# A W4 macaron block on one core: gate and up scale and zero tables loaded in TensorE's row layout, the first layer norm in halves

## The chip, the cores and the metric

One core of a Trainium2 chip runs the whole program. The metric is the device time of one execution in microseconds (us), as the median of several runs. TensorE (PE in the rows, PEld for its weight loads), VectorE (DVE), ScalarE (ACT), GpSimd (POOL) and the queue of SyncE (SP) each work through their own instructions in order and wait for each other on semaphores. A trailing q, as in SPq or ACTq, marks what a sequencer does itself, above all issuing a DMA.

## What is computed

The input x is 2048 tokens of 512 numbers. It passes a feed-forward block, an attention layer and the same feed-forward block again, each behind a layer norm and each added back:

```python
x = x + 0.5 * ffn(layernorm(x))
x = x + attn(layernorm(x))
x = x + 0.5 * ffn(layernorm(x))
```

The feed-forward weights are 4-bit numbers, eight in one int32, with one scale and one zero for each group of 128 input rows and each output column:

```python
w = (qw[:, None, :] >> shifts[None, :, None] & 15).reshape(-1, n)        # HID 512, INTER 1376
z = ((qz[:, :, None] >> shifts[None, None, :] & 15) + 1).reshape(groups, -1)
W = (w - z[g_idx]) * scales[g_idx]
h = silu(xf @ Wg) * (xf @ Wu)
out = h @ Wd
```

Gate and up have 4 groups (GK), down has 10 (GD). The index g_idx may name any group for any input row, so a row's scale has to be looked up.

## The kernel before

**Where the work is.** The 2048 rows are four blocks of 512 for the two feed-forward passes. Block 0 and block 1 of the first pass ("pair 0") go through plain_top and plain_bottom. While plain_top runs, the weights are unpacked too. All matrix products are made of three passes over a high and a low part of each number, so a 128x512 product over 512 input rows is 12 matmuls.

**Units.** The weights are unpacked in 33 units, a unit being one 128-column tile of gate (m = 0) or up (m = 1), or one 128-row tile of down (m = 2). Their order is gate 0, up 0, then for every i from 1 gate i, up i, down i-1. Gate and up have 11 tiles (NT). For unit u:

- the queue brings the packed words into the tile qs (load_units, L490), VectorE shifts and masks them in place (unpack, L1703)
- TensorE makes the zeros and scales of the unit with scales_zeros(u) (L816 for gate and up, L814 for down): a one-hot matrix oh_gu or oh_d times a table tab_gu or tab_d. This waits until VectorE is done with unit u-1 (s_wf)
- dequantise(u) on VectorE subtracts the zeros (wi, L1619) and multiplies by the scales (wf, L1720)
- ScalarE copies wf to the high part (w_hi, L1245) and GpSimd makes the low part (w_lo, L2109). TensorE may then multiply with it (s_wlo)

**The tables.** A table has for each matrix 3 rows per group with the three bf16 parts of the scale, and from row 32 on one row per group with the zeros. Up's rows start at 64 (FOLD). Before, scales and zeros are loaded spread over many partitions (sc_gu, zq_gu), GpSimd cuts the scales in three parts (cut_scales, 5 instructions), VectorE unpacks the zeros (unpack_zeros, 8 shifts and one sum), and 8 DMAs of the SP queue (table, L418 and L421) carry the pieces across partitions into tab_gu. Down's tables take the same way, with the zeros unpacked by VectorE as its first work.

**The start.** In program order TensorE does keep_warm(4), that is 4 products of the identity that nobody reads, scales_zeros(0), the turning of x's first two 128-row tiles (L1030), scales_zeros(1), the other two, scales_zeros(2) and keep_warm(4), and then plain_top. keep_warm is at L743 and waits at the start for the identity and the column shift (d_small). VectorE makes the layer norm's statistics (ln_stats, ln_var), GpSimd the power -1/2 (deviation), ScalarE applies it (ln_apply, L1250).

**plain_top on TensorE.** For every tile i: 12 matmuls of gate, scales_zeros(3i+2), 12 of up, scales_zeros(3i+3), 12 of down for tile i-1, scales_zeros(3i+4). VectorE does dequantise(3i+2), the product with silu (hs, L1745), dequantise(3i+3), the low part of hT, dequantise(3i+4). For i = 0 VectorE has units 2 to 5 in it, and the one-hot of down's first tile; for i = 1 the one-hot of the other tiles (128x640). GpSimd prepares these one-hots between its w_lo of units 2 and 4 (L452, L455).

## Time and profile before

| | us |
|---|---|
| median of 3 runs | 856.06 |
| lowest and highest | 855.16, 857.8 |
| the profiled execution | 854.81 |
| its span, as in the page | 853.0 |
| TensorE busy in that span | 829.8 |

The profiled execution has 1.81 us outside its span. A row of the timeline is: start, duration, engine, line, operation, output<-inputs, shapes, count, and in brackets how long the engine had been idle and what ended that. Rows of the same kind are merged, and a merged duration runs from the first start to the last end.

### The profile page before, as it was taken

The numbers are of one execution on the slowest core, as the hardware profiler recorded it, in microseconds if no ns is written. First come the engines' busy times: TensorE is split into PE (matmuls) and PEld (weight loads), VectorE is DVE, ScalarE is ACT, GpSimd is POOL, SyncE is SP. The second block draws the span as 40 slices with busy tenths as digits, with TensorE's granted clock in tenths as the row PEclk, the third lists the DMA queues.
The fourth block names the chain that finished last, engine by engine and source line by source line (L and its number), as shares of the span: only waits on it lengthen the run. The fifth ranks groups of instructions, "written<-read, shape, count | busy, mean of one in ns | idle before, by whom it ended". The sixth has DMA issues, their size and how long they took to land.

```text
span 853.0 us, 10668 instructions
## 1 busy us (share of the span) xinstructions
PE 829.8 (97%) x4004; PEld 674.2 (79%) x4004; DVE 481.9 (56%) x798; ACT 272.3 (32%) x469; POOL 243.8 (29%) x198
## 2 busy tenths in 40 slices
PE   2999999999999999999999999999999999999998
PEld 2777768887888888788888888888888888888786
DVE  4877655564845444464967786545445744434452
ACT  2323332354421121241574783111212512111221
POOL 4544431563210533030235362150510201101100
PEclk9999999999999999999999999999999999999999
DMA  6767556995484534152115156845345063544121
GB/s 153 215 231 245 185 178 229 337 325 209 171 313 136 173 127 147 50 161 88 61 68 179 50 172 247 309 136 173 125 149 165 22 226 132 163 146 153 35 100 50
DMA packets 72290, 139.37 MB, mean 163 GB/s; under 512 B 25566, under 2 KB 36494, under 8 KB 67246
## 3 DMA queue, kind: packets, MB, share of 16 engines
q1 hardware_dynamic: 66236, 130.79, 45.6%
q10 hardware_dynamic: 5874, 7.48, 2.8%
q8 instruction: 32, 0.52, 0.3%
q0 software_dynamic: 128, 0.41, 0.3%
q14 instruction: 20, 0.16, 0.1%
HBM read 100.54 MB, written 37.95 MB: 162 GB/s over the span
## 4 chain that ended last, share of the span: by engine, by line
PE 73%; DVE 2%; ACT 1%; issue 0%; POOL 0%; DVEq 0%; ACTq 0%; POOLq 0%
PE ps L729 37%; PE ps L736 33%; PE ps L747 2%; PE ps L1130 1%; DVE xn L1651 1%; DVE pT L1619 0%; ACT pr L1479 0%; POOL t L2109 0%; ACT oT L1245 0%; DVE oT L1619 0%; DVE t L1619 0%; DVE hT L1619 0%; PE ps L1056 0%; DVE mx L1946 0%; ACT xn L1250 0%
## 5 line engine op out<-in xcount | busy, mean ns | idle before, releaser
L729 PE MATMUL ps<-blk,ring 128*128 128x512 f32 (+1 forms) x1386 | 320.9, 389 | 0.1
L729 PEld LDWEIGHTS ps<-blk,ring 128*128 128x128 f32 (+1 forms) x1386 | 256.7, 185 | 58.1 <-DVE blk L1619 0.5
L736 PE MATMUL ps<-wd,hT 128*128 128x512 f32 (+1 forms) x1056 | 251.1, 392 | 0.9 <-DVE hT L1619 0.8
L736 PEld LDWEIGHTS ps<-wd,hT 128*128 128x128 f32 (+1 forms) x1056 | 196.8, 188 | 43.8 <-DVE hT L1619 1.2
L2151 POOL TENSOR_TENSOR h<-h,u 128x512 f32<-128x512 f32 (+1 forms) x33 | 42.7, 1293 | 326.0 <-ACT h L1372 326.0
L736 PE MATMUL ps<-xT,wp 128*128 128x512 f32 x480 | 115.8, 396 | 0.0
L736 PEld LDWEIGHTS ps<-xT,wp 128*128 128x128 f32 x480 | 88.5, 188 | 21.2 <-issue 2.0
L1622 DVE TENSOR_TENSOR u<-ps,p1s 128x512 f32<-128x512 f32 (+1 forms) x66 | 45.4, 687 | 97.3 <-PE ps L729 97.3
L1372 ACT ACTIVATE h<-h 128x512 f32<-128x512 f32 (+1 forms) x33 | 20.9, 632 | 176.8 <-DVE h L1622 176.8
L1622 DVE TENSOR_TENSOR u<-ps,u 128x512 f32<-128x512 f32 (+1 forms) x66 | 45.6, 691 | 25.7 <-PE ps L729 24.6
L1622 DVE TENSOR_TENSOR h<-ps,p1s 128x512 f32<-128x512 f32 (+1 forms) x33 | 22.8, 691 | 64.1 <-PE ps L729 64.1
L1619 DVE TENSOR_TENSOR hT<-h,hT 128x512 fp32r<-128x512 f32 (+1 forms) x44 | 30.7, 712 | 24.8 <-ACT hT L1245 24.8
L1367 ACT ACTIVATE g<-ps 128x512 f32<-128x512 f32 (+1 forms) x33 | 19.7, 598 | 76.1 <-PE ps L729 76.1
L1245 ACT ACTIVATE hT<-u 128x512 fp32r<-128x512 f32 (+1 forms) x33 | 20.9, 632 | 64.4 <-DVE u L1835 64.4
L1835 DVE TENSOR_TENSOR u<-u,g 128x512 f32<-128x512 f32 (+1 forms) x33 | 38.8, 1174 | 1.1
L2119 POOL TENSOR_SCALAR xn<-xn,mv,rstd 128x512 f32<-128x512 f32 x18 | 38.3, 2136 | 0.5
L1245 ACT ACTIVATE hT<-h 128x512 fp32r<-128x512 f32 (+1 forms) x44 | 27.0, 629 | 35.5 <-PE ps L736 35.5
L2109 POOL TENSOR_TENSOR wp<-wf,wp 128x512 fp32r<-128x512 f32 x20 | 26.9, 1344 | 40.1 <-ACT wp L1245 40.0
L1619 DVE TENSOR_TENSOR hT<-u,hT 128x512 fp32r<-128x512 f32 (+1 forms) x33 | 22.8, 692 | 23.0 <-ACT hT L1245 23.0
L2114 POOL TENSOR_TENSOR rstd<-rstd,mhalf 128x4 f32<-128x4 f32 x12 | 15.2, 1267 | 66.9 <-DVE rstd L1640 66.9
L1619 DVE TENSOR_TENSOR wi<-qs,ps 128x512 bf16<-128x512 int32 (+2 forms) x33 | 22.3, 676 | 19.1 <-PE ps L816 13.8
L1860 DVE SCALAR_TENSOR_TENSOR xres<-ps,xres 128x512 f32<-128x512 f32 x32 | 21.6, 689 | 18.6 <-PE ps L736 18.5
(123 smaller groups left out, 876.7 us busy)
## 6 DMA issues: line engine op xcount, KB each, us to landing
ring<-wsaved SPq DMA_DIRECT2D x29, 1024.0 KB, 5.1
ring<-wsaved SPq DMA_DIRECT2D x33, 768.0 KB, 4.4
wsaved<-wp SPq DMA_DIRECT2D x10, 1024.0 KB, 4.7
stream<-xres SPq DMA_DIRECT2D x32, 256.0 KB, 2.2
xn<-stream SPq DMA_DIRECT2D x8, 1024.0 KB, 7.8
xres<-stream SPq DMA_DIRECT2D x32, 256.0 KB, 4.0
wfull<-wf ACTq DMA_DIRECT2D x20, 256.0 KB, 3.3
wsaved<-wp SPq DMA_DIRECT2D x10, 512.0 KB, 3.0
```

Source lines behind the costliest of these rows:

```text
L729: mm = pe.matmul(ps[0:w, bank, :], ring[:, slot, which, a, kt, 0:w], blk[:, which, b, kt, :], start=not onto and kt == 0 and n == 0, stop= ...
L736: mm = pe.matmul(bank_ap, lhs(a), rhs(b), start=first and n == 0, stop=last and n == 2)
L1245: return act.activation(dst, src, ACT.Copy)
L1367: act.activation(g1[0:w, n % 2, :], ps[0:w, product_bank(n // NT + 1, 0), :], ACT.Silu).then_inc(s_g1, 1)
L1372: act.activation(hidden(i)[0:width(i), :], hidden(i)[0:width(i), :], ACT.Silu).then_inc(s_g2, 1)
L1619: return dve.tensor_tensor(out=dst, in0=a, in1=b, op=ALU.subtract)
L1622: return dve.tensor_tensor(out=dst, in0=a, in1=b, op=ALU.add)
L1835: dve.tensor_tensor(out=u2[0:w, n % 2, :], in0=u2[0:w, n % 2, :], in1=g1[0:w, n % 2, :], op=ALU.mult)\
L1860: dve.scalar_tensor_tensor(out=xres[:, r, :], in0=ps[:, down_bank(q, half, r), :], scalar=0.5, in1=xres[:, r, :], op0=ALU.mult, op1=ALU.ad ...
L2109: return pool.tensor_tensor(out=dst, in0=a, in1=b, op=ALU.subtract)
L2119: pool.tensor_scalar(x_rows(t)[:, r, :], x_rows(t)[:, r, :], mv[:, t % 2, r, 0:1], rstd[:, t % 2, r:r + 1], ALU.subtract, ALU.mult).then_i ...
L2151: pool.tensor_tensor(out=hidden(i)[0:w, :], in0=hidden(i)[0:w, :], in1=u3[0:w, n % 2, :], op=ALU.mult).then_inc(s_h2, 1)
```

## The change

**Loads.** The SP queue now loads the indices first, then zq_gu as 4 rows for each matrix straight into the rows of the table, and sc_gu three times over as 12 rows for each matrix. GpSimd clears both tiles first, and SP waits for that. The rows between are thus zero.

**Tables made in place.** VectorE makes the tables in three pieces of columns: tiles 0 and 1 (256 columns) at the start, tiles 2 to 4 (384) in plain_top with i = 0, tiles 5 to 10 (736) with i = 2. For a piece, zeros_gu is 8 shifts and one sum on 100 partitions, and scales_gu two scalar_tensor_tensor on 76 partitions. They subtract the upper half of the float, or not, by a constant keep for each row, and TensorE reads the upper 16 bits of what is left (upper, a step of two bf16). The 8 table DMAs for gate and up are gone, and GpSimd's 5 cuts for them too. TensorE waits for a piece (s_tab) ahead of the first unit of its tiles.

**Down.** Unpacking down's zeros moves from VectorE's first work to plain_top, i = 0, behind the first one-hot. Its DMA into tab_d follows that. GpSimd's clamp and compare for down move from the start to just ahead of w_lo(2).

**The start.** Normalising x's first block goes in halves on VectorE, GpSimd and ScalarE. TensorE makes 12 warm-up products at the start instead of 4, turns all four tiles of x in one go, makes scales_zeros(1) and scales_zeros(2) behind them, and the 4 warm-up products ahead of plain_top are gone. ScalarE's queue brings unit 0 right behind x, and SP's brings unit 1.

```diff
-        def unpack_zeros(eng, step, sc, rest, rest2, parts, zq, zi, zb):
+        def unpack_zeros(eng, step, zq, zi, zb):
...
+        def scales_gu(eng, step, piece):
...
+            first, end = TAB_TILES[piece][0] * P, min(TAB_TILES[piece][1] * P, INTER)
+            s, left, dst = sc_gu[S_ROWS, first:end], left_gu[S_ROWS, 0:end - first], tab_gu[S_ROWS, first:end]
+            step(lambda: eng.scalar_tensor_tensor(out=left, in0=upper(s), scalar=keep[S_ROWS, 0:1], in1=s,
+                                                  op0=ALU.mult, op1=ALU.subtract))
+            step(lambda: eng.scalar_tensor_tensor(out=dst, in0=upper(left), scalar=keep[S_ROWS, 1:2], in1=left,
+                                                  op0=ALU.mult, op1=ALU.subtract))
...
             sp.dma_start(idt[:, :], ident).then_inc(d_small, 16)
             sp.dma_start(shift[:, :], shifts).then_inc(d_small, 16)
-
-
-            for j in range(3):
-                sp.wait_ge(s_cut, 2 * j + 1)
-                for m in range(2):
-                    table(sp, m, pieces=(j,))
-            sp.wait_ge(s_tab, 2 * ZERO_STEPS)
-            for m in range(2):
-                table(sp, m, pieces=(3,))
+            load_units(sp, [1])
+            sp.dma_start(zq_d, flat(zeros[2], ZC_D)).then_inc(d_zq_d, 16)
             load_units(sp, [2, 3])
-            sp.wait_ge(s_cut, 2 * CUT_STEPS)
-            table(sp, 2)
+            sp.wait_ge(s_cut, CUT_STEPS)
+            table_d(sp, 0, range(3))
             load_units(sp, [4, 5])
+            sp.wait_ge(s_tab, ZEROS_D_DONE)
+            table_d(sp, 0, (3,))
...
+                if m == 0:
+                    for piece, (first, _) in enumerate(TAB_TILES):
+                        if i == first:
+                            pe.wait_ge(s_tab, TAB_DONE[piece])
...
             pe.wait_ge(d_small, 32)
-            keep_warm(4)
-
-            pe.wait_ge(d_tab[0], 64)
-            pe.wait_ge(s_oh, 3)
+            keep_warm(12)
+
+            pe.wait_ge(s_oh, 2)
             scales_zeros(0)
             for r in range(RT):
-                if r == 2:
-                    pe.wait_ge(d_tab[1], 64)
-                    scales_zeros(1)
                 pe.wait_ge(s_ln[0], r + 1)
...
+            scales_zeros(1)
             scales_zeros(2)
-            keep_warm(4)
...
                     if i == 0:
-                        dve.wait_ge(s_ohd, 2)
+                        dve.wait_ge(s_ohd, 3)
                         one_hot(dve, hots, DOWN_FIRST, 1, oh_d[:, 0:P])
+                        unpack_zeros(dve, tables, zq_d, zi_d, zb_d.rearrange("p c j -> p (c j)"))
                         dequantise(3)
...
+                    if i == 2:
+                        zeros_gu(dve, tables, 2)
+                        scales_gu(dve, tables, 2)
...
                     if i == 0:
                         dequantise(4)
+                        zeros_gu(dve, tables, 1)
+                        scales_gu(dve, tables, 1)
                         dequantise(5)
```

VectorE in plain_top, i = 0, from unit 4 on, before (wi and wf belong to dequantise, qs to unpack, hs and hT to the hidden tile):

```order
L1619 TENSOR_TENSOR hT<-hs,hT 128x512
L1619 TENSOR_TENSOR wi<-qs,ps 128x512
L1720 TENSOR_TENSOR wf<-wi,ps 128x512
L1703 TENSOR_SCALAR qs<-qs,shift 128x512
L1619 TENSOR_TENSOR wi<-qs,ps 128x512
```

The same stretch now:

```order
L1653 TENSOR_TENSOR hT<-hs,hT 128x512
L1653 TENSOR_TENSOR wi<-qs,ps 128x512
L1756 TENSOR_TENSOR wf<-wi,ps 128x512
L1739 TENSOR_SCALAR qs<-qs,shift 128x512
L460 TENSOR_SCALAR zi_gu<-zq_gu 100x48 x8
L462 TENSOR_SCALAR zb_gu<-zi_gu 100x384
L474 SCALAR_TENSOR_TENSOR left_gu<-sc_gu,keep 76x384
L476 SCALAR_TENSOR_TENSOR tab_gu<-left_gu,keep 76x384
L1653 TENSOR_TENSOR wi<-qs,ps 128x512
```

Eleven instructions stand between dequantise(4) and dequantise(5). The same eleven, with 92 and 736 columns, stand ahead of the hs of i = 2.

The SP queue from the constants on, before:

```order
L574 DMA idt<-in_ident 128x128
L575 DMA shift<-in_shifts 128x1
L418 DMA tab_gu<-parts_gu 4x32x43 x6
L421 DMA tab_gu<-zb_gu 4x4x344 x2
L490 DMA qs<-in_L_ffn_gate_qweight 128x1x128 x4
L490 DMA qs<-in_L_ffn_up_qweight 128x1x128 x4
L418 DMA tab_d<-parts_d 10x8x64 x3
L421 DMA tab_d<-zb_d 10x4x128
L490 DMA qs<-in_L_ffn_down_qweight 128x1x512
```

The same stretch now, behind the loads of idx, grp, zq_gu and sc_gu:

```order
L612 DMA idt<-in_ident 128x128
L613 DMA shift<-in_shifts 128x1
L522 DMA qs<-in_L_ffn_up_qweight 128x1x128 x4
L615 DMA zq_d<-in_L_ffn_down_qzeros 40x16
L522 DMA qs<-in_L_ffn_gate_qweight 128x1x128 x4
L522 DMA qs<-in_L_ffn_up_qweight 128x1x128 x4
L423 DMA tab_d<-parts_d 10x8x64 x3
L522 DMA qs<-in_L_ffn_down_qweight 128x1x512
L522 DMA qs<-in_L_ffn_gate_qweight 128x1x128 x4
L426 DMA tab_d<-zb_d 10x4x128
```

The transfers that VectorE's and GpSimd's cuts fed are gone from the front, and the one with down's zeros stands behind two more units.

## Rows read from the trace of the kernel before

**Rows 1.** The page: busy time by engine, share of the span and count.
```profile
PE 829.8 (97%) x4004; PEld 674.2 (79%) x4004; DVE 481.9 (56%) x798; ACT 272.3 (32%) x469; POOL 243.8 (29%) x198
```
**Rows 2.** Stretches: start:end, length, busy us by engine, granted clock, DMA share, GB/s.
```profile
35.00:45.00 10.00, 9.33 (x53) 6.87 (x46) 9.48 (x13) 3.40 (x6) 5.54 (x5) 1.00 0.97 309
45.00:115.00 70.00, 70.00 (x388) 49.63 (x386) 50.03 (x88) 24.09 (x39) 29.69 (x23) 1.00 0.69 228
```
**Rows 3.** The only wait of TensorE in 24.7 to 125 us: total, times, longest.
```profile
PE ps L814 <- DVE wf L1720: 0.7, 1, 0.7
```
**Rows 4.** Timeline of the start: tables and layer norm.
```profile
6.21 0.88 DVE L446 TENSOR_SCALAR zi_gu<-zq_gu 32x43 int32<-32x43 int32 x8 [0.41 <-DMA zq_gu<-in_L_ffn_up_qzeros]
7.12 0.33 DVE L448 TENSOR_SCALAR zb_gu<-zi_gu 32x344 bf16<-32x344 int32 x1
...
10.06 1.29 POOL L2114 TENSOR_TENSOR rstd<-rstd,mhalf 128x4 f32<-128x4 f32 x1 [1.16 <-DVE rstd L1640]
10.22 3.25 SPq L421 DMA_DIRECT2D tab_gu<-zb_gu  x2
...
11.53 0.74 DVE L458 SCALAR_TENSOR_TENSOR oh_gu<-idf,grp,oh_gu 128x512 bf16<-128x512 f32 x1
11.65 2.92 ACT L1250 ACTIVATE xn<-xn,nmr,rstd 128x512 f32<-128x512 f32 x4 [5.67 <-DVE nmr L1644]
```
**Rows 5.** Timeline of TensorE up to plain_top.
```profile
9.33 2.08 PE L743 MATMUL ps<-idt 128*128 128x128 f32 x8 [9.33 <-DMA shift<-in_shifts]
17.56 0.61 PE L816 MATMUL ps<-tab_gu,oh_gu 4*128 4x128 bf16 x8 [6.16 <-DMA tab_gu<-zb_gu]
20.54 1.97 PE L1030 MATMUL ps<-idt,xn 128*128 128x128 f32 x8
22.98 2.01 PE L743 MATMUL ps<-idt 128*128 128x128 f32 x8
24.71 4.41 PE L736 MATMUL ps<-xT,wp 128*128 128x512 f32 x18
```
**Rows 6.** Timeline: warm-ups and turning at another pace, later.
```profile
30.89 0.60 PE L743 MATMUL ps<-idt 128*128 128x128 f32 x4
127.82 1.04 PE L747 MATMUL ps<-idt,xn 128*128 128x128 f32 x8
```
**Rows 7.** Timeline of plain_top, i = 0 and 1: VectorE, GpSimd, TensorE.
```profile
20.72 0.69 DVE L1619 TENSOR_TENSOR wi<-qs,ps 128x512 bf16<-128x512 int32 x1 [0.64 <-PE ps L816]
24.56 1.28 POOL L2109 TENSOR_TENSOR wp<-wf,wp 128x512 fp32r<-128x512 f32 x1 [2.79 <-ACT wp L1245]
24.93 1.19 DVE L1703 TENSOR_SCALAR qs<-qs,shift 128x512 int32<-128x512 int32 x1
27.88 0.35 DVE L458 SCALAR_TENSOR_TENSOR oh_d<-idf,grp,oh_d 128x128 bf16<-128x128 f32 x1
34.03 0.69 DVE L1720 TENSOR_TENSOR wf<-wi,ps 128x512 f32<-128x512 bf16 x1
34.78 0.40 PE L816 MATMUL ps<-tab_gu,oh_gu 4*128 4x128 bf16 x8
38.00 1.90 DVE L458 SCALAR_TENSOR_TENSOR oh_d<-idf,grp,oh_d 128x640 bf16<-128x640 f32 x1
42.40 3.02 PE L736 MATMUL ps<-xT,wp 128*128 128x512 f32 x12
```
**Rows 8.** Timeline of i = 2.
```profile
47.19 0.48 DVE L1703 TENSOR_SCALAR qs<-qs,shift 128x512 int32<-128x512 int32 x1
48.02 1.28 POOL L2109 TENSOR_TENSOR wp<-wf,wp 128x512 fp32r<-128x512 f32 x1 [1.74 <-ACT wp L1245]
48.77 0.69 DVE L1745 TENSOR_TENSOR hs<-hs,ps 128x512 f32<-128x512 f32 x1 [1.10 <-PE ps L736]
50.09 0.69 DVE L1720 TENSOR_TENSOR wf<-wi,ps 128x512 f32<-128x512 bf16 x1
51.98 0.39 PE L814 MATMUL ps<-tab_d,oh_d 10*128 10x512 bf16 x2
```

More of the change, by code:

```diff
@@ L252, in macaron @@
         d_q = [sem(f"d_q{n}") for n in range(QSLOTS)]
-        d_tab = [sem(f"d_tab{n}") for n in range(4)]
+        d_tab = [sem(f"d_tab{n}") for n in range(2)]
         d_full = [sem(f"d_full{n}") for n in range(2)]
@@ L407, in spread, with table_d, upper @@
             return indices.rearrange("(o n) -> o n", o=1).to_broadcast([FOLD, indices.shape[0]])
-        def table(eng, m, at_row=0, pieces=range(4)):
-            if m == 2:
-                (_, _, _, parts, _, _, zb), dst, g, done = cuts[1], tab_d, GD, d_tab[3 if at_row else 2]
-            else:
-                (_, _, _, parts, _, _, zb), dst, g, done, at_row = cuts[0], tab_gu, GK, d_tab[m], FOLD * m
-                parts, zb = parts[:, :, m * SC:(m + 1) * SC], zb[m * ZP:(m + 1) * ZP, :, :]
+        def table_d(eng, at_row, pieces=range(4)):
+            done = d_tab[1 if at_row else 0]
             for j in [j for j in pieces if j < 3]:
-                eng.dma_start(dst[at_row + j * g:at_row + (j + 1) * g, :], parts[:, j, :]).then_inc(done, 16)
+                eng.dma_start(tab_d[at_row + j * GD:at_row + (j + 1) * GD, :], parts_d[:, j, :]).then_inc(done, 16)
             row = at_row + Z_ROW
             if 3 in pieces:
-                eng.dma_start(dst[row:row + g, :], zb.rearrange("p c j -> p (c j)")).then_inc(done, 16)
+                eng.dma_start(tab_d[row:row + GD, :], zb_d.rearrange("p c j -> p (c j)")).then_inc(done, 16)
+        def upper(ap):
+            return ap.bitcast(BF16)[:, 1::2]
         def maker(eng, semaphore):
@@ L595, in _ @@
                 if u == 9:
[L596 removed]
+                    table_d(sp, FOLD)
                 if u == 12:
@@ L815, in scales_zeros @@
                         else:
+                            cols = slice(i * P, i * P + w)
                             mm = pe.matmul(ps[:, bank, k * P:k * P + w], oh_gu[rows, k * P:(k + 1) * P],
-                                           tab_gu[rows, i * P:i * P + w], start=True, stop=True)
+                                           zb_gu[rows, cols] if bank == Z_BANK else upper(tab_gu[rows, cols]),
+                                           start=True, stop=True)
                 mm.then_inc(s_sz, 1)
@@ L1251, in ln_apply, with rows_hi @@
                                    scale=rstd[:, t % 2, r:r + 1]).then_inc(s_ln[t], 1)
-            def rows_hi(t):
-                for k in range(KT):
+            def rows_hi(t, kts=range(KT)):
+                for k in kts:
                     act.wait_ge(s_turn, KT * t + k + 1)
```

172 lines of the change are left out of this document (101 added, 71 removed).

## The prediction

> **What bounds the kernel now.** I read the page's busy times first: TensorE is busy for 829.8 of the 853.0 us of the span [rows 1], so the time is TensorE's, and what can be won is where it stands still, 23 us in all. Its timeline and the list of its waits say where: 9.33 us ahead of its first instruction, 6.16 us for the last piece of gate's table [rows 5], and 0.7 us for VectorE in plain_top [rows 3]. The table by stretches then tells who is near the limit behind the start. From 45 to 115 us TensorE is busy for 70.00 of 70.00 us and VectorE for 50.03; from 35 to 45 us it is the other way about, with VectorE at 9.48 of 10 us and TensorE at 9.33 [rows 2]. So there are two questions. When does the first product of plain_top start (24.71 us now [rows 5]), and does VectorE keep up behind it, now that it is to make the tables there?
>
> **The start.** Now TensorE does its warm-ups at 9.33 us and then waits for a table until 17.56 us [rows 5]. The table is late since SP issues its last two transfers from 10.22 us on for 3.25 us [rows 4], and they have to land. These go away. What is late next is, in turn:
>
> The constants. The first warm-up waits for the shift, which is there at 9.33 us [rows 5]. In the new order SP has 256 KB of indices and the scales, three times over, in front of it and waits for two memsets of GpSimd, which no row shows; on the other hand 6 of the 8 table transfers no longer crowd in behind it. I take 9.3 us again, from 8.5 to 10.5.
>
> The warm-ups. Four take 2.08 us at the start (8 records [rows 5]) and two take 0.60 us later (4 records [rows 6]), so 12 take 6.2 us at the slow pace and 3.6 at the fast one. The eight records ahead of plain_top still take 2.01 us at 22.98 us [rows 5]: the clock is at the lower of its two levels (1.2 GHz) until plain_top, although the granted clock reads 1.00 in all rows. I take 5.7 us, most of them slow, and so 15.0 us for the end of the warm-ups.
>
> VectorE and ScalarE are ready by then. For piece 0 VectorE has 8 shifts (0.88 us for 43 columns, so no more for 32) and a sum (0.33 us for 344 columns, 0.29 for 256 [rows 4]), and two scalar_tensor_tensor. Their price is that of the one-hot: 0.74 us for 512 columns [rows 4], which with VectorE's other one (0.35 us for 128 columns [rows 7]) makes 0.21 us and 1.04 ns for each column, so 0.48 us for 256. With statistics, one-hot and waits this ends near 12.5 us. The second power of GpSimd (1.29 us [rows 4]) ends near 12, and ScalarE's four tiles (2.92 us [rows 4]) near 14.2 us.
>
> Then scales_zeros(0), 0.5 us, and 16 turnings. They take 1.97 us for 8 at the slow pace [rows 5] and 1.04 at the fast one [rows 6]: I take the fast one, 2.1 us, since TensorE has been busy for 6 us without a gap, and keep the slow one (1.9 us more) for the range. With scales_zeros(1) VectorE's dequantise(1) starts at about 18.1 us. Before, it started at 20.72 us [rows 7]. The first product came 3.99 us after that, held back by the four warm-ups in front of it. Now it only waits for the first row tile's low part: 0.72 + 0.61 + 0.69 + 0.1 = 2.1 us, so 20.2 us. **The start gives 4.5 us.**
>
> **The tables in plain_top, i = 0.** Now dequantise(4) ends at 34.03 + 0.69 = 34.72 us, and scales_zeros(5) starts at 34.78 us [rows 7]: already here TensorE follows VectorE. In the new program scales_zeros(5) is the first that reads piece 1, so it waits for eleven more instructions, and what is queued behind it are gate's, up's and down's products. VectorE's chain from the start of dequantise(1), from start to start in the rows' durations: wi and wf 1.33, four low parts of x 2.48, unpack(2) 0.48, dequantise(2) with unpack(3) 1.81, one-hot 0.35, down's zeros 0.97 (8 shifts and a sum, as they take now at the start), dequantise(3) 1.81, hs and hT with ScalarE's copy between them 2.07, dequantise(4) 1.81, zeros of piece 1 1.2 (8 times 0.1, and 0.36 for 384 columns), its scales 1.25 (2 times 0.61). The sum is 15.6 us.
>
> This chain has no slack that takes waits for GpSimd in. A row shows what such a wait is: the unpack at 24.93 us takes 1.19 us instead of 0.48, and it ends at 26.12, that is 0.28 us after GpSimd's w_lo of 24.56 to 25.84 us; the one-hot at 38.00 us takes 1.90 us [rows 7] instead of 0.88. So such an instruction of VectorE waits for the w_lo that is under way. A w_lo starts some 0.8 us after its wf ends (48.02 us, behind an unpack that started at 47.19 us as wf ended [rows 8]), and for units 2 and 4 that is now in the midst of the new instructions. The bounds are 0 (they just miss) and 3.3 us (three w_lo of 1.28 us, less 0.5 us that they overlap anyhow). I take 1.9 us, nearer to the upper end, since with units 2 and 4 the times fall together by the sum. **Piece 1 is ready 17.5 us after dequantise(1), at 35.6 us, and scales_zeros(5) starts at 35.7 us, 0.9 us later than now.** The 4.5 us are gone: TensorE has done what it can 10.1 us after its first product (34.78 - 24.71 [rows 5, 7]), at 30.3 us, and stands still for some 5.3 us.
>
> Down's table is not what is late. Its zeros are ready at about 26.5 us, the transfer takes some 2.1 us to land (bounds 2 and 4.5 us, the table transfers of the start), and scales_zeros(4) is due at 28.3 us. Up to 2 us of wait there would only shorten the wait behind it.
>
> Behind it, before, TensorE needs 42.40 - 34.78 = 7.62 us to gate's product of i = 2, of which 0.7 us is a wait for VectorE [rows 3, 7], whose long one-hot came ahead of hs. Now VectorE has that one-hot done while TensorE is still in up's products, and I take 0.2 us for the rest of the wait: 35.7 + 7.15 = 42.85 us. **At i = 2 the kernel stands 0.45 us later than before.**
>
> **The tables at i = 2.** The third piece is 8 shifts of 92 words (0.11 us each), a sum (0.53 for 736 columns) and two scalar_tensor_tensor (0.98 each): 3.5 us with their gaps. They stand between the unpack at 47.19 us and hs at 48.77 us, where VectorE is idle for 1.10 us. Behind hs, dequantise(9) ends at 50.78 us, 1.20 us ahead of scales_zeros(10) at 51.98 us [rows 8]. So 2.3 us are covered and 1.2 us are not. With GpSimd's w_lo of unit 8 in it, at about 48 us, it is 2.2 us. I take 1.6 us. All later pieces of work have their cover: VectorE has 50.03 us of work in 70 us [rows 2]. **Here 1.6 us are lost.**
>
> **Sum.** +0.45 + 1.6 = +2.0 us against the profiled execution of 854.81 us. That execution lies 1.25 us below the median of 856.06 us, and I put the difference on the median: 858.1 us, 0.2% more. Differences within 0.3% (2.6 us) are about what a measurement of this kernel can't tell from no change.
>
> **Rivals.**
>
> *The clock falls in the new wait (slower).* Up to 24.7 us rows show TensorE at its lower level, after it stood still from 11.41 to 17.56 us [rows 5]; no row has it stand still for more than 0.7 us once it is at 2.4 GHz [rows 3]. The new wait for piece 1 is about 5.3 us, in the midst of plain_top. If the clock falls there, the same work takes twice as long until it rises again. TensorE worked at the slow pace from 17.56 to 24.7 us [rows 5] before it ran fast, so I price it with 2 to 7 us of slow work, of which half is lost, 1.0 to 3.5 us, and take 2.5: 860.6 us. It decides by the wait at scales_zeros(5): one of 0.7 us leaves the clock up, one of 5.3 us may not. The Trainium skill says on the page TensorE: Matmul & The Clock Gate, in the section "Why this matters for your kernels", that gaps in TensorE's work between bursts of matmuls bring it back to the lower clock; by that page the forecast would be this rival and not the even case, while no run here shows it yet.
>
> *VectorE is through earlier (faster).* If the new instructions miss GpSimd's w_lo and the constants land at 8.5 us, the table is ready at 32.9 us instead of 35.6 us, and at i = 2 1.2 us are lost instead of 1.6. That would be -3 us; with one of the two, -1. I take 854.6 us, from 851.5 to 856.3. For it speaks that the rows have only one such wait for certain between 24 and 30 us [rows 7].
>
> *The start stays slow.* The turning of x at the slow pace makes all of it 1.9 us later, or the constants land after 10.5 us: 860 us. A table read in steps of two bf16 that slowed its 4 products in each unit would also give this: one product is 0.40 / 8 = 0.05 us [rows 7], so 0.2 us in each of some 17 units, 3.4 us.
>
> **How the numbers follow.** Even case with its 2.0 us: 40%, of which 27% end within 2.6 us. The clock falls: 20%, nearly all of it slower. VectorE through earlier: 30%, 17% below -2.6 us and 13% within. Slow start or slow table: 10%, 8% slower. Together faster 17%, the same 43%, slower 40%. The range leaves out about a tenth at each end: 853.0 to 862.0 us.
>
> **What the changed profile would show.** First product of plain_top at about 20 us. TensorE waits for VectorE at scales_zeros(5) for 4 to 6 us, with the eleven instructions at 30 to 36 us. The warm-ups of the start change their pace within the twelve. gate's product of i = 2 at about 43 us, and ahead of scales_zeros(10) a wait of 1 to 2 us. The busy time of TensorE behind 55 us is as before. The prediction is wrong if the wait at scales_zeros(5) is under 2 us, if the first product starts after 22 us, or if products behind that wait run at half their pace.

## The result: 0.6% slower, and the profile after

The changed kernel takes 862.09 us in the median of 4 runs (862.04 to 862.29), the kernel before 856.81 us beside it (4 runs, 855.16 to 857.8): a ratio of 1.0064 with a 95% interval of 1.0046 to 1.0082. It is slower by 5.3 us. The forecast was 858.1 us, and the time lies just outside its range, whose upper end was 862.0 us. Nothing in the forecast's likeliest case had the size of this; the nearest case was the first rival, the falling clock, at 860.6 us.

The profiled execution after is one of 862.04 us, 7.2 us above the one of before (854.81 us); the working below is against that one. First its page's busy times, and all waits of TensorE in the first 130 us (total, times, longest):

```profile
PE 833.5 (97%) x4012; PEld 677.5 (79%) x4012; DVE 486.7 (57%) x824; ACT 272.4 (32%) x469; POOL 248.7 (29%) x202
```

```profile
PE ps L776 <- DMA shift<-in_shifts: 11.0, 1, 11.0
PE ps L854 <- DVE tab_gu L476: 4.6, 1, 4.6
PE ps L851 <- DVE wf L1756: 2.3, 1, 2.3
PE ps L854 <- DVE wf L1756: 1.6, 1, 1.6
PE ps L769 <- DVE xT L1653: 0.3, 1, 0.3
```

The 6.16 us of wait for a table at the start [rows 5] are gone. In their place there are 4.6 us for VectorE's table work at scales_zeros(5), 2.3 us at scales_zeros(10), and 1.6 us at scales_zeros(2), where before the only wait in plain_top was one of 0.7 us [rows 3]. TensorE is also busy for 3.7 us more than before [rows 1], of which the 4 more products of the identity explain 0.6 us (12 in 4.71 us, 8 in 2.08 + 2.01 us before [rows 5]). The timeline of TensorE tells why (warm-ups L776, turnings L1065, products L769, scales_zeros L854 and L851):

```profile
11.04 4.71 PE L776 MATMUL ps<-idt 128*128 128x128 f32 x24 [11.04 <-DMA shift<-in_shifts]
16.01 1.97 PE L1065 MATMUL ps<-idt,xn 128*128 128x128 f32 x16
20.57 5.97 PE L769 MATMUL ps<-xT,wp 128*128 128x512 f32 x18 [0.29 <-DVE xT L1653]
...
36.82 0.28 PE L854 MATMUL ps<-zb_gu,oh_gu 4*128 4x128 bf16 x1 [4.62 <-DVE tab_gu L476]
37.35 5.19 PE L769 MATMUL ps<-xT,wp 128*128 128x512 f32 x12
42.81 3.02 PE L769 MATMUL ps<-wd,hT 128*128 128x512 f32 x12
46.08 3.06 PE L769 MATMUL ps<-xT,wp 128*128 128x512 f32 x12
57.99 0.39 PE L851 MATMUL ps<-tab_d,oh_d 10*128 10x512 bf16 x2 [2.30 <-DVE wf L1756]
```

The first product starts at 20.57 us instead of 24.71 us [rows 5], so the new start is worth 4.1 us. But its first 18 matmuls take 5.97 us, where they took 4.41 us [rows 5], and the 12 of up's product at 37.35 us take 5.19 us, where such a product takes 3.02 us elsewhere. The table by stretches has the reason in its column for the granted clock (the last but two):

```profile
21.60:25.00 3.40, 3.40 (x10) 2.63 (x9) 3.30 (x11) 0.00 (x0) 1.68 (x3) 0.50 0.49 139
25.00:35.20 10.20, 7.19 (x39) 4.92 (x37) 8.05 (x26) 3.49 (x6) 8.49 (x5) 1.00 0.49 146
35.30:42.00 6.70, 5.18 (x19) 4.04 (x20) 4.00 (x6) 0.63 (x1) 1.99 (x2) 0.50 0.76 249
42.10:59.10 17.00, 14.70 (x81) 10.26 (x81) 14.06 (x28) 4.39 (x7) 4.82 (x4) 1.00 0.60 193
59.20:62.50 3.30, 3.30 (x10) 2.52 (x8) 1.41 (x3) 0.63 (x1) 2.15 (x2) 0.50 0.45 118
```

TensorE works at 1.2 GHz (0.50) in three stretches: from 21.6 us, shortly after the wait of 1.6 us; from 35.3 us, in the wait of 4.6 us; and from 59.2 us, shortly after the wait of 2.3 us. Before, the clock reads 1.00 from the first product to 35 us, and behind that too [rows 2]:

```profile
24.70:35.00 10.30, 10.30 (x60) 7.53 (x59) 8.10 (x14) 2.63 (x5) 6.97 (x5) 1.00 0.68 200
```

VectorE's eleven instructions for piece 1, and GpSimd beside them:

```profile
32.05 0.96 DVE L1739 TENSOR_SCALAR qs<-qs,shift 128x512 int32<-128x512 int32 x1
32.93 0.85 DVE L460 TENSOR_SCALAR zi_gu<-zq_gu 100x48 int32<-100x48 int32 x8
33.82 0.75 DVE L462 TENSOR_SCALAR zb_gu<-zi_gu 100x384 bf16<-100x384 int32 x1
34.60 1.51 DVE L474 SCALAR_TENSOR_TENSOR left_gu<-sc_gu,keep 76x384 f32<-76x384 bf16 x1
36.15 0.61 DVE L476 SCALAR_TENSOR_TENSOR tab_gu<-left_gu,keep 76x384 f32<-76x384 bf16 x1
...
31.94 2.41 POOL L483 TENSOR_SCALAR oh_d<-idf,grp 128x640 bf16<-128x640 f32 x1
34.44 1.26 POOL L2156 TENSOR_TENSOR wd<-wf,wd 128x512 fp32r<-128x512 f32 x1
```

left_gu takes 1.51 us and tab_gu 0.61 us for the same 384 columns. The first of them ran beside GpSimd's w_lo of 34.44 to 35.70 us.

**Where 7.2 us come from.** Step by step along TensorE's path, in us, profiled executions:

| | before | after | grows by |
|---|---|---|---|
| scales_zeros(5) starts | 34.78 | 36.82 | 2.0 |
| from there to gate's product of i = 2 | 7.62 | 9.26 | 1.6 |
| wait at scales_zeros(10) | none | 2.30 | 2.3 |
| gate's product of i = 3 | 3.06 | 4.61 | 1.6 |

That is 7.5 us, against 7.2 us at the end. The second row hides a part of the clock's price: the 7.62 us before hold the wait of 0.7 us [rows 3], and the 9.26 us after hold none. So TensorE's own work on that way grew by 2.3 us, 2.2 us of it in up's product (5.19 against 3.02 us). With the 1.6 us of the last row the lower clock costs 3.9 us in this execution. Behind it nothing changes: from 125 us to 850 us TensorE is busy for 721.39 us of 725 after and for 720.97 us before.

### The profile page after: what moved, and what is told of

It reads as the page before. It is cut to its first block, busy times and chain, and to the rows that moved or that the text cites. A ratio compares the mean times of both kernels' runs of the same rounds, so it can differ in the third digit from the quotient of the medians.

```text
span 860.2 us, 10709 instructions
## 1 busy us (share of the span) xinstructions
PE 833.5 (97%) x4012; PEld 677.5 (79%) x4012; DVE 486.7 (57%) x824; ACT 272.4 (32%) x469; POOL 248.7 (29%) x202
## 4 chain that ended last, share of the span: by engine, by line
PE 72%; DVE 2%; ACT 1%; issue 0%; POOL 0%; DVEq 0%; ACTq 0%; POOLq 0%
PE ps L762 36%; PE ps L769 33%; PE ps L780 2%; PE ps L1165 1%; DVE xn L1687 1%; DVE pT L1653 0%; ACT pr L1513 0%; POOL t L2156 0%; ACT oT L1280 0%; DVE oT L1653 0%; DVE t L1653 0%; DVE hT L1653 0%; PE ps L1091 0%; DVE mx L1993 0%; ACT xn L1285 0%
## 5 line engine op out<-in xcount | busy, mean ns | idle before, releaser
L769 PE MATMUL ps<-wd,hT 128*128 128x512 f32 (+1 forms) x1056 | 250.8, 392 | 0.8 <-DVE hT L1653 0.7
L769 PEld LDWEIGHTS ps<-wd,hT 128*128 128x128 f32 (+1 forms) x1056 | 196.8, 188 | 43.5 <-DVE hT L1653 1.1
L769 PE MATMUL ps<-xT,wp 128*128 128x512 f32 x480 | 120.8, 409 | 0.3 <-DVE xT L1653 0.3
L769 PEld LDWEIGHTS ps<-xT,wp 128*128 128x128 f32 x480 | 92.4, 196 | 22.9 <-issue 2.7
L2161 POOL TENSOR_TENSOR rstd<-rstd,mhalf 128x4 f32<-128x4 f32 (+1 forms) x13 | 15.5, 1196 | 67.5 <-DVE rstd L1675 67.5
L1902 DVE SCALAR_TENSOR_TENSOR xres<-ps,xres 128x512 f32<-128x512 f32 x32 | 21.6, 690 | 18.8 <-PE ps L769 18.5
```

The lines of the kernel that those rows point to most:

```text
L769: mm = pe.matmul(bank_ap, lhs(a), rhs(b), start=first and n == 0, stop=last and n == 2)
L1902: dve.scalar_tensor_tensor(out=xres[:, r, :], in0=ps[:, down_bank(q, half, r), :], scalar=0.5, in1=xres[:, r, :], op0=ALU.mult, op1=ALU.ad ...
```

## Experiments

Two theories are on trial. *A: the new waits for table work and the lower clock behind them are the whole loss.* *B: a part of it lies in something else: the new start, the table read in steps of two, or waits that turn up wherever the work is put.* The kernels before ran on the same chips: 855.11 us (7 runs) beside the first four, 855.34 us (29) beside the next four, 855.82 us (18) beside the last three. The intervals in the table are those of the ratios to these. The changed kernel wasn't run again beside them: its ratio is to the 856.81 us of its own 4 runs, and the later medians of the kernel before are 1.0 to 1.7 us lower. So a difference of two medians and a difference of two ratios don't say the same, and where it matters both are given. One of e10_fill's ten executions took 2816.43 us, for a reason that no run shows; the ratio leaves it out, and without it the median is 858.54 us.

| run | median us | ratio, 95% | first product | scales_zeros(5) | wait there | lower clock (us) |
|---|---|---|---|---|---|---|
| changed kernel | 862.09 | 1.0046 to 1.0082 | 20.57 | 36.82 | 4.62 | 3.4 + 6.8 + 3.4 |
| e1_warm_wait | 860.76 | 1.0049 to 1.0112 | 21.18 | 37.43 | 1.53 | 3.4 + 3.5 |
| e2_warm_start | 862.65 | 1.0074 to 1.0116 | 21.09 | 37.59 | 5.64 | 6.8 + 3.4 |
| e3_split_last | 861.29 | 1.0058 to 1.0098 | 21.33 | 37.84 | 5.65 | 6.9 |
| e4_zd_front | 861.87 | 1.0068 to 1.0107 | 21.05 | 37.31 | 4.63 | 3.4 + 6.9 + 3.5 |
| e5_spread | 856.43 | 1.0001 to 1.0025 | 20.94 | 32.54 | none | 3.4 + 3.4 |
| e6_warm_zd | 859.35 | 1.0032 to 1.0071 | 21.94 | 36.62 | 4.68 | 6.8 + 3.4 |
| e10_fill | 858.70 | 1.0024 to 1.0050 | 20.90 | 37.70 | 0.74 | 3.5 |
| e11_early_hot | 859.91 | 1.0028 to 1.0069 | 21.36 | 35.69 | 3.99 | 6.8 + 3.4 |
| e8_best | 852.65 | 0.9960 to 0.9985 | 18.94 | 28.98 | none | none |
| e9_slots | 849.77 | 0.9918 to 0.9951 | 20.75 | 30.80 | none | none |

Marks and stretches are from the one profiled execution of each run; "lower clock" lists how long each stretch at 1.2 GHz lasted. The shift lands between 9.4 and 11.8 us from run to run, so marks of two runs compare to some 0.5 us only.

### The clock alone: warm-up products in the waits

```diff
+                    if i == 1:
+                        warm(14, 7)
                     scales_zeros(3 * i + 2)
```

> The changed kernel with 14 more warm-up products (into a bank that is free then) ahead of scales_zeros(5), so that TensorE is busy while it waits for piece 1 of the tables; nothing else is changed. Theory A (the clock falls because TensorE stands still for 4.6 us there, and that costs time): the granted clock stays at 1.00 from 35 to 42 us, the way from scales_zeros(5) to gate's product of i = 2 shrinks from 9.26 us to 7.1 to 7.3 us, and the time falls by about 2 us, to 860.0 us. Theory B (only the wait itself costs; the slow work of TensorE lies beside VectorE's): the clock stays up, but gate's product of i = 2 starts at 46.0 us as before and the time stays at 862.1 us. In both, piece 1 is ready at 36.8 us.

Products of the identity fill two thirds of the wait. The clock falls later and for half as long, for 3.5 us; gate's product of i = 2 comes 8.43 us behind scales_zeros(5) instead of 9.26 us. In this execution the clock also stayed up behind the wait of 2.29 us at i = 2, which the edit doesn't touch: gate's product of i = 3 takes 3.06 us instead of 4.61 us.

```profile
58.09 3.06 PE L769 MATMUL ps<-xT,wp 128*128 128x512 f32 x12
```

The median of 860.76 us is 1.3 us below the changed kernel's, but the four executions reach from 859.4 to 863.73 us and the interval of the ratio overlaps that of the changed kernel, so this run alone shows no gain. A wait of 1.53 us was still left. So both waits were then filled nearly whole:

```diff
+                    if i == 1:
+                        warm(20, 7)
                     scales_zeros(3 * i + 2)
...
+                        if i == 2:
+                            pe.wait_ge(s_silu, 3)
+                            warm(10, 0)
                         scales_zeros(3 * i + 4)
```

> The changed kernel with 20 warm-up products ahead of scales_zeros(5) and 10 ahead of scales_zeros(10), so that both waits are filled nearly whole; the tables are where the change put them. This takes the lower clock away and leaves the waits. Theory A (behind the two waits the clock costs 1.6 us each): scales_zeros(5) and scales_zeros(10) start when VectorE is done, as in the changed kernel, granted clock 1.00 from 25 us on, gate's product of i = 2 7.0 to 7.6 us behind scales_zeros(5) instead of 9.3 us, and 3 us less in all, 859 us. Theory B (what follows the waits is slow for another reason, or warm-ups don't hold the clock): low clock in the same places and 862 us, or more, since the warm-ups overrun the waits.

```profile
26.00:60.00 34.00, 32.77 (x204) 25.52 (x202) 27.64 (x54) 8.33 (x14) 16.01 (x11) 1.00 0.62 201
```

The clock is 1.00 from 26 to 60 us, gate's product of i = 2 comes 6.89 us behind scales_zeros(5) (44.59 - 37.70), and that of i = 3 takes 3.04 us. Together that is 2.4 + 1.6 = 4.0 us less, about the 3.9 us worked out above. The median falls by 3.4 us to 858.7 us, with VectorE's work just where the change put it; by the ratios it is 2.3 us (1.0037 against 1.0064). So the clock behind the two waits costs 2.3 to 4 us, and theory A's 3 us lie within. The remaining 2.9 us above the kernel before (858.70 against 855.82 us) fit the waits themselves.

### VectorE's chain: what makes piece 1 late

```diff
             scales_zeros(1)
+            warm(5, 0)
             scales_zeros(2)
```

> The changed kernel with 5 more warm-up products between scales_zeros(1) and scales_zeros(2), where TensorE waits 1.6 us for VectorE. Theory A (the low clock of 21.6 to 25.0 us comes from the thin work of TensorE between the warm-ups and the first product, and it holds VectorE up by 1.3 us at dequantise(3)): the clock stays at 1.00 until the long wait, the first 18 matmuls take 4.5 us instead of 5.97, piece 1 is ready at 35.5 us instead of 36.8, and the time is 860.8 us. Theory B (the slow products lie in the shadow of VectorE, which is the bound): piece 1 is ready at 36.8 us again and the time stays at 862.1 us.

The lower clock behind the first product goes, and the first 18 matmuls take 4.36 us. It gains nothing at all: scales_zeros(5) starts no earlier and waits 1.0 us longer. The trace shows why. VectorE's wait of 1.28 us for TensorE ahead of dequantise(3) is gone, but the eight shifts of down's zeros take 2.36 us instead of 0.73 us. GpSimd's low part falls among them now, at 25.39 us; in the changed kernel it starts at 26.45 us, behind them:

```profile
25.26 2.36 DVE L460 TENSOR_SCALAR zi_d<-zq_d 40x16 int32<-40x16 int32 x8
...
25.39 1.28 POOL L2161 TENSOR_TENSOR wp<-wf,wp 128x512 fp32r<-128x512 f32 x1 [1.40 <-ACT wp L1285]
```

So 1.28 us are won and 1.6 us lost. Neither of the two theories of this run had that. Down's zeros alone, unpacked at the start again:

```diff
+            dve.wait_ge(d_zq_d, 16)
+            unpack_zeros(dve, tables, zq_d, zi_d, zb_d.rearrange("p c j -> p (c j)"))
             dve.wait_ge(d_zq_gu, 32)
             zeros_gu(dve, tables, 0)
```

> The changed kernel with down's zeros unpacked at the start again, while VectorE waits for gate's and up's zeros (their load goes ahead of theirs). Theory A (VectorE's chain from dequantise(1) to piece 1 is the bound, every instruction in it counts): piece 1 is ready 1.0 us earlier after dequantise(1), at 35.8 us, and the time falls by 1 us to 861.1 us, if the start isn't held up. Theory B (TensorE's slow products set the chain: VectorE waits 1.28 us for them at dequantise(3)): VectorE just waits 2.2 us there, piece 1 is ready at 36.8 us and the time stays at 862.1 us.

Nothing either: scales_zeros(5) starts at 37.31 us, since VectorE now waits 2.29 us instead of 1.28 us for scales_zeros(3), behind TensorE's slow first 18 matmuls. Each of the two edits hides the other's gain: without the warm-ups VectorE waits for TensorE, and with them down's zeros meet GpSimd. Together:

> The changed kernel with five warm-up products between scales_zeros(1) and scales_zeros(2) and with down's zeros unpacked in the start again; piece 1 stays where it is. Theory A (VectorE's own chain from dequantise(1) to piece 1 sets the end of the wait; its idle 1.3 us ahead of dequantise(3) came from TensorE at the lower clock, and down's zeros cost 1.0 us more): piece 1 is ready 16.0 to 16.5 us after the start of dequantise(1) instead of 18.3 us, scales_zeros(5) at 35 to 35.5 us with a wait of 4 to 5 us, and the lower clock behind it stays: about 860 us. Theory B (each relief is eaten by a wait for GpSimd's low parts, which the chain then meets elsewhere): still 18 us or more, and 862 us.

Piece 1 is ready 16.8 us after the start of dequantise(1) (19.79 to 36.56 us) instead of 18.3 us, and the median is 859.35 us. On the same chip that is 3.3 and 2.5 us less than with either edit alone. Against the changed kernel it is 2.7 us less by the medians and 1.1 us by the ratios (1.0051 and 1.0064). The expected 16.0 to 16.5 us was missed a little: VectorE still waits 0.66 us for TensorE. On top of this, GpSimd's 640 columns of one-hot were moved ahead of its low parts of units 2 and 3, away from piece 1:

```diff
                     compare_low(pool, hots, DOWN_FIRST, 1, oh_d[:, 0:P])
-                if u == 3:
                     clamp(pool, hots, DOWN_REST, GD)
-                if u == 4:
+                if u == 3:
```

> The changed kernel with five warm-up products between scales_zeros(1) and scales_zeros(2), down's zeros in the start, and one more move: GpSimd prepares the one-hot of 640 columns ahead of its low parts of units 2 and 3 instead of those of units 3 and 4, so that it doesn't work beside VectorE's unpacking for unit 5 and the eleven instructions of piece 1. Theory A (VectorE's instructions that take 0.97 instead of 0.48, 0.75 instead of 0.36 and 1.51 instead of 0.61 us wait for GpSimd's instruction under way): without the comparison beside them two of the three are back at the short time, piece 1 is ready 15.3 to 16.0 us after the start of dequantise(1) instead of 16.8 us, and scales_zeros(5) starts 1 us earlier. Theory B (they are slow for what they read or write, or for DMA traffic): their times stay.

```profile
31.57 0.48 DVE L1744 TENSOR_SCALAR qs<-qs,shift 128x512 int32<-128x512 int32 x1
31.97 1.96 DVE L460 TENSOR_SCALAR zi_gu<-zq_gu 100x48 int32<-100x48 int32 x8
33.97 0.36 DVE L462 TENSOR_SCALAR zb_gu<-zi_gu 100x384 bf16<-100x384 int32 x1
34.37 0.61 DVE L474 SCALAR_TENSOR_TENSOR left_gu<-sc_gu,keep 76x384 f32<-76x384 bf16 x1
...
32.40 1.38 POOL L2161 TENSOR_TENSOR wd<-wf,wd 128x512 fp32r<-128x512 f32 x1 [0.91 <-ACT wd L1285]
```

Three instructions are back at their short times (0.48, 0.36 and 0.61 us). But w_lo(4) now starts at 32.40 us, and the eight shifts, 0.85 us before, take 1.96 us: each long one runs beside a GpSimd instruction. Such an overlap isn't enough by itself: in the changed kernel the eight shifts of 32.93 us take 0.85 us beside GpSimd's comparison of 31.94 to 34.35 us. The whole shrinks by 0.3 us only, less than the 0.8 to 1.5 us expected, and 859.91 us can't be told from 859.35 us. The waits for GpSimd move with the work; they aren't a property of these instructions. The Trainium skill has this as a rule (SBUF — State Buffer, section "Who interferes with whom"): VectorE and GpSimd share a pair of ports as an exclusive lock. A VectorE instruction in a two-port mode contends for it, and so does one with two SBUF inputs against a GpSimd one that reads SBUF. By that rule the trace agrees for left_gu, which has two inputs in SBUF, at 1.51 against 0.61 us; for the shifts, which have one, no run here shows in which mode they ran.

### The last piece in two

```diff
-        TAB_TILES = ((0, 2), (2, 5), (5, NT))
+        TAB_TILES = ((0, 2), (2, 5), (5, 8), (8, NT))
...
-                    if i == 2:
-                        zeros_gu(dve, tables, 2)
-                        scales_gu(dve, tables, 2)
+                    if i in (2, 6):
+                        zeros_gu(dve, tables, 2 if i == 2 else 3)
+                        scales_gu(dve, tables, 2 if i == 2 else 3)
```

> The changed kernel with the last piece of the tables (tiles 5 to 10, 736 columns, at i = 2) cut in two: tiles 5 to 7 at i = 2, tiles 8 to 10 at i = 6. Theory A (the piece is longer than the 2.3 us in which VectorE is idle or ahead; the rest is TensorE's wait, and the clock falls after it): the wait of 2.3 us ahead of scales_zeros(10) shrinks to about 1 us, no low clock follows at 59 us, a wait of up to 1 us comes at i = 6, and the time is 859.0 to 860.0 us. Theory B (it is the 22 instructions that cost, not the length of the piece): 22 instead of 11 are as dear, time 862 us or more.

```profile
58.56 0.39 PE L851 MATMUL ps<-tab_d,oh_d 10*128 10x512 bf16 x2 [1.39 <-DVE wf L1756]
58.88 1.45 PE L769 MATMUL ps<-xT,wp 128*128 128x512 f32 x5
```

The wait of 2.30 us is now one of 1.39 us at i = 2 and one of 1.38 us at i = 6, so the waits sum to no less. Behind neither of them does the clock fall (from 44.3 to 62 us it is 1.00). Whether that is due to the shorter waits is open, since it didn't fall behind 2.29 us in e1_warm_wait either. The start of this kernel is that of the changed one, and yet the clock stayed up behind its wait of 1.57 us at scales_zeros(2):

```profile
20.64 0.23 PE L854 MATMUL ps<-zb_gu,oh_gu 4*128 4x128 bf16 x1 [1.57 <-DVE wf L1756]
21.33 4.35 PE L769 MATMUL ps<-xT,wp 128*128 128x512 f32 x18 [0.29 <-DVE xT L1653]
```

As in e2_warm_start, down's zeros then take 2.35 us beside GpSimd, and scales_zeros(5) starts 1.0 us later than in the changed kernel, of which the later first product is 0.8 us. The median is 0.8 us below the changed kernel's, the ratio is above its (1.0078 and 1.0064): no gain is shown.

### The tables spread over plain_top

The same work, cut otherwise: tiles 0 to 3 at the start, the rest ahead of the hidden products of i = 1 to 4.

```diff
-        TAB_TILES = ((0, 2), (2, 5), (5, NT))
+        TAB_TILES = ((0, 4), (4, 7), (7, NT))
...
-                    if i == 2:
-                        zeros_gu(dve, tables, 2)
-                        scales_gu(dve, tables, 2)
+                    if i in (1, 3):
+                        zeros_gu(dve, tables, 1 if i == 1 else 2)
+                    if i in (2, 4):
+                        scales_gu(dve, tables, 1 if i == 2 else 2)
...
                         dequantise(4)
-                        zeros_gu(dve, tables, 1)
-                        scales_gu(dve, tables, 1)
                         dequantise(5)
```

> The changed kernel with its tables cut elsewhere: tiles 0 to 3 (512 columns) at the start, where VectorE was idle for 1.41 us, tiles 4 to 6 and 7 to 10 in four pieces of work of about 1.3 us ahead of the hidden products of i = 1 to 4. The same work as in the changed kernel, nowhere in TensorE's way. Theory A (the whole loss is table work that TensorE waits for at scales_zeros(5) and at i = 2, and the lower clock behind both waits): no wait above 1 us at scales_zeros(5) or scales_zeros(10), granted clock 1.00 from 25 us on, scales_zeros(5) at about 33 us after a first product at about 21 us, gate's product of i = 3 6 to 8 us earlier than in the changed kernel, and 853 to 856 us in all. Theory B (a part of the loss sits in the tables' new form or in the new start, so cutting them elsewhere doesn't help): waits gone, but still above 858 us. Theory C (the pieces of work only move the waits to i = 1 to 4): four waits of about 1 us, 857 to 860 us.

856.43 us, 5.7 us less than the changed kernel (4.4 us by the ratios), though the first product starts no earlier. That is 0.4 us above theory A's 853 to 856 us, and gate's product of i = 3 comes 5.3 us sooner (53.00 against 58.31 us), not 6 to 8 us. scales_zeros(5) starts at 32.54 us, 4.3 us sooner, without a wait. The tables' new form costs nothing that shows: a unit's four products take as long as before. Theory C of this run is partly true: ahead of scales_zeros(7) a wait of 1.96 us stands in for the old ones, and behind it the clock falls once more, for 3.4 us:

```profile
41.15 0.39 PE L851 MATMUL ps<-tab_d,oh_d 10*128 10x512 bf16 x2 [1.96 <-DVE wf L1756]
41.47 4.61 PE L769 MATMUL ps<-xT,wp 128*128 128x512 f32 x12
```

### The start of the kernel before, without its last warm-ups

```diff
             scales_zeros(2)
-            keep_warm(4)
             plain_top()
```

> The kernel before without the four warm-up products ahead of plain_top, a part of the change alone. If these four (2.0 us at the slow pace) only stand in front of the first product, it starts at about 23.3 us instead of 24.7 us, and VectorE, which waits 1.36 us for scales_zeros(3), has it 1.4 us earlier: scales_zeros(5) at 33.4 us instead of 34.8 us and 1.0 to 1.4 us less in all. If they hold the clock up, the first 18 matmuls take 6 us instead of 4.4 us as in the changed kernel, and the two cancel: no difference above 0.3 us.

856.35 us in 10 runs (852.57 to 857.59), a ratio of 1.0005 (0.9987 to 1.0022). The first product starts 5.81 us behind scales_zeros(0) (18.63 to 24.44 us) instead of 7.15 us [rows 5], so the four do stand in the way, for 1.3 us, and the first 18 matmuls take 4.36 us without them, so they don't hold the clock. In the profiled execution scales_zeros(0) itself came 1.1 us later, so scales_zeros(5) started at 34.51 us and not at the 33.4 us expected. The median shows no gain, and the times scatter over 5 us, so what this is worth in all stays unclear.

### A version that beats both

e8_best adds to e5_spread the five warm-up products between scales_zeros(1) and scales_zeros(2), down's zeros as VectorE's first work, and other orders at the start (the lines are against e5_spread; the warm-ups and down's zeros are as in the diffs above):

```diff
+            sp.dma_start(idt[:, :], ident).then_inc(d_small, 16)
+            sp.dma_start(shift[:, :], shifts).then_inc(d_small, 16)
             sp.wait_ge(s_cst, 2)
...
-            ln_stats(0, (0,))
-            dve.wait_ge(d_zq_gu, 32)
-            zeros_gu(dve, tables, 0)
-            ln_stats(0, (1,))
+            ln_stats(0, (0, 1))
             ln_var(0, (0, 1))
             ln_stats(0, (2, 3))
             ln_shift(0, (0, 1))
             ln_var(0, (2, 3))
+            dve.wait_ge(d_zq_gu, 32)
+            zeros_gu(dve, tables, 0)
+            ln_shift(0, (2, 3))
```

> The tables cut as in the run with tiles 0 to 3 first, five warm-up products between scales_zeros(1) and scales_zeros(2), down's zeros as VectorE's first work, identity and shift loaded ahead of gate's and up's scales, and the statistics of all four row tiles ahead of the zeros. Theory A: the constants land at about 9.5 us, first product at 19.5 to 20 us without a lower clock behind it, scales_zeros(5) at 29.5 to 30.5 us, and from there as in the kernel before, 4 to 5 us earlier: 850 to 853 us, faster than both. Rival: SP's and ScalarE's weight loads can't follow (the DMA engines are 0.97 busy from 35 to 45 us already in the kernel before), VectorE waits for packed words at units 6 to 10, and 2 us or more of it are lost: 853 to 856 us.

852.65 us, 0.28% less than before. The first product starts at 18.94 us and scales_zeros(5) at 28.98 us, both half a microsecond ahead of theory A, but of the 5.8 us that it is early, waits of 1.96, 0.82, 0.20, 0.53 and 0.58 us give some back; the longest stands again at scales_zeros(7). The wait of 0.98 us that VectorE has for a save of wf at 43.08 us is the only sign of the rival, the transfers. The last version takes more of the table work out of TensorE's way (the lines are against e8_best; the order of the loads, zeros first, is left out):

```diff
-                    if i == 1:
-                        dve.wait_ge(s_ohd, 5)
-                        one_hot(dve, hots, DOWN_REST, 1, oh_d[:, P:D_COLS])
...
                                       op=ALU.mult).then_inc(s_h, 1)
+                    if i == 1:
+                        dve.wait_ge(s_ohd, 5)
+                        one_hot(dve, hots, DOWN_REST, 1, oh_d[:, P:D_COLS])
...
                     else:
                         dequantise(3 * i + 4)
+                    if i in (1, 2, 4, 5):
+                        scales_gu(dve, tables, 1 if i < 3 else 2, (0,) if i in (1, 4) else (1,))
...
             dve.wait_ge(d_zq_gu, 32)
             zeros_gu(dve, tables, 0)
+            zeros_gu(dve, tables, 1)
```

> The version with tiles 0 to 3 first, and three more moves: gate's and up's zeros are loaded first of all and all of them unpacked at 3.5 to 7 us, where VectorE had 2.65 us of idle time; the four scalar_tensor_tensor of tiles 4 to 10 stand one by one at the end of i = 1, 2, 4 and 5, where VectorE waits for scales_zeros anyhow; the one-hot of 640 columns stands behind the hidden product of i = 1. In the version before it TensorE still waited 1.96, 0.82, 0.20, 0.53 and 0.58 us for VectorE. Theory A (these waits are VectorE's work ahead of the hidden product, lengthened by GpSimd's low parts): they are gone or under 0.3 us each, first product at 19 to 19.8 us, 849 to 850.5 us. Rival: the start pays, since the unpacking delays the statistics of x and with them the turning: first product at 20.5 us or later, 851 to 853 us.

```profile
PE ps L776 <- DMA shift<-in_shifts: 10.1, 1, 10.1
PE ps L858 <- DVE tab_gu L477: 1.0, 2, 0.5
PE ps L769 <- DVE xT L1659: 0.3, 1, 0.3
PE ps L858 <- DVE wf L1762: 0.3, 1, 0.3
```

```profile
14.00:125.00 111.00, 109.36 (x617) 78.88 (x617) 83.11 (x143) 38.11 (x64) 52.61 (x43) 1.00 0.67 209
```

849.77 us, 0.66% below the kernel before (0.9918 to 0.9951) and 11 to 12 us below the changed one, by ratios and by medians. The first product starts at 20.75 us, 0.2 us later than in the changed kernel: the start is not what separates them. TensorE waits 1.6 us in all behind its first instruction, and the granted clock is 1.00. So the rival's mark of this run came true (the start is 1.8 us later than in e8_best), but not its time, since the waits that went weigh more. Theory A had the time (849 to 850.5 us) and most of the waits, though not the first product, and two waits of 0.5 us for table work are left. With the long waits and the lower clock away, scales_zeros(5) starts at 30.80 us instead of 34.78 us, so the new start's 4 us are kept. This version has several edits at once, and no run says what each of them is worth.

## Why the prediction was wrong

**What bounds the kernel** was right: TensorE, with VectorE close behind it in plain_top.

**The constants** landed at 11.04 us, not 9.3 us, and outside the 8.5 to 10.5 us allowed. SP issued the shift only at 5.50 us, behind eight other loads. By that, the third rival's condition (constants after 10.5 us, 860 us) was met, but its price was not: the miss was mostly covered by luck. The warm-ups took 4.71 us instead of 5.7 us and changed pace within the twelve, and the turnings took 1.97 us, about as said. dequantise(1) started at 18.42 us (18.1), the first product at 20.57 us (20.2).

**The chain to piece 1** took 18.3 us instead of 17.5 us. The price of GpSimd's waits was right: 0.48 (unpack), 0.05 (shifts), 0.39 (sum) and 0.90 us (left_gu) over the times that the forecast counted make 1.8 us, where 1.9 was taken. What was left out is VectorE's idle time of 1.28 us ahead of dequantise(3), for scales_zeros(3), which stands behind TensorE's slow first matmuls. The forecast had counted VectorE's chain as if it never waited for TensorE. The rest of the chain was some 0.4 us shorter than counted, so only 0.8 us of it show. With the constants this made scales_zeros(5) 1.1 us later than the 35.7 us forecast.

**"No row has it stand still for more than 0.7 us once it is at 2.4 GHz": the step that failed is the choice between the even case and the first rival.** The forecast itself found a new wait of 5.3 us (measured: 4.62) and gave a fall of the clock in it only 20%. It did fall, and the runs with filled waits show that it costs. The even case put the clock at nothing on the ground of waits of up to 0.7 us; measured, it costs 3.9 us. The rival's mechanism was right and also incomplete. It was priced at 2.5 us in one place; it took 2.3 us there, and another 1.6 us behind the wait at i = 2, which the forecast had found (1.6 us) and never asked about the clock. The forecast's own sign of being wrong, products at half their pace behind that wait, came true. A third fall, from 21.6 us on, cost 1.6 us of TensorE's time too (5.97 against 4.41 us), of which nothing arrived at the end by itself: in e2_warm_start it is away, and VectorE's chain meets GpSimd instead. The sentence of the Trainium skill named in the rival (TensorE: Matmul & The Clock Gate, section "Why this matters for your kernels"), that gaps in TensorE's work between bursts of matmuls bring it back to the lower clock, was the better guide for the long wait: the trace agrees, with 0.50 from 35.3 us on. For the two shorter waits the runs themselves go both ways (see the last section).

**The wait at i = 2** was 2.30 us instead of 1.6 us. The work took 4.6 us (51.30 to 55.89 us) instead of 3.5 us: the sum over 736 columns took 1.46 us where 0.53 was counted, beside a low part of GpSimd of 51.73 to 53.46 us.

**The sum.** +2.0 us was forecast against the profiled execution and +7.2 us came: 1.1 us at scales_zeros(5), 2.1 us on the way to gate's product of i = 2 (9.26 instead of 7.15 us), 0.7 us of wait and 1.6 us of clock at i = 2, in all 5.5, of which 5.2 show at the end. More than half of it is the clock. The case of VectorE through earlier was wrong, its instructions did meet GpSimd's. It was also mis-summed: with the table ready at 32.9 us and 1.2 us lost at i = 2, its terms give 33.0 + 7.15 - 42.40 + 1.2 = -1.05 us against the kernel before. The -3 us are the distance from the even case, and the 17% given to a gain of more than 2.6 us had no ground in it. The strided table cost nothing that shows. TensorE's busy time is as before only behind 62.5 us, not behind 55 us, since the last slow stretch lies between.

## What to carry to other kernels

A wait that an edit puts into a busy TensorE costs its own length and then the slow work behind it: here 4.6 + 2.3 us of wait drew 3.9 us of clock, more than half as much again. Before moving work from a DMA to an engine, look for that engine's idle time ahead of each consumer: the same table work cost 7 us in two places, and spread over VectorE's gaps in e9_slots TensorE waits 1.0 us for it. Where two engines follow each other closely, a relief for one can push its work into another's way (here 1.28 us won and 1.6 us lost), so read the trace for what the relief met, and try two reliefs together before calling either useless.

## What the runs showed of the hardware

- The length of a wait alone did not tell whether the clock falls. It fell behind waits of 1.53, 1.57, 1.96, 2.30 us, and behind every wait of 3.99 us and more in plain_top. It did not behind 1.38, 1.39 and 1.57 us in e3_split_last, nor behind 2.29 us in e1_warm_wait; waits of the same 1.57 and 2.30 us at the same places drew it down in the changed kernel. It did not behind one of 1.96 us in e8_best either, where the row of that stretch reads 1.00:

```profile
37.60:48.00 10.40, 9.93 (x54) 7.07 (x54) 8.03 (x13) 3.02 (x5) 4.02 (x3) 1.00 0.86 295
```

- It also differs between executions of one program. Of e8_best's twelve, six have a mean granted clock of 0.998 and take 852.74 to 853.15 us; the other six have 0.999 or 1.000 and take 851.62 to 852.55 us. The profiled one is of the second kind, so "none" in the table is true of it and not of all. A stretch of 3.4 us at half the clock would make 0.002 of 850 us (an estimate from the stretches above).
- The stretches at 1.2 GHz behind the waits of 1.53 to 2.30 us lasted 3.3 to 3.5 us, those behind waits of 3.99 us and more 6.7 to 6.9 us, the first part of them still in the wait.
- Eight small shifts of 100x48 take 0.85 us together, and 1.96 us when one GpSimd instruction of 1.38 us falls among them (e11_early_hot); eight of 40x16 take 0.73 us, and 2.36 us with one of 1.28 us (e2_warm_start).
- The kernel before scatters from 852.4 to 858.1 us over 29 runs on one chip, so that one profiled execution of it is no sharper than some 3 us as a base for the time.
